# The projection to dt, B and C spread over the in-projection's blocks, and the dt blocks behind the first x and z block

## The reference, cut to what matters

```python
xn = (xf - mu) * rsqrt(var + EPS) * ln_w + ln_b       # LayerNorm over 512 channels
xz = xn @ in_proj_w.T                                 # 512 -> 2 x 1024
xin, z = split(xz, 2)
xs = silu(causal_depthwise_conv(xin, 4 taps) + conv_b)
x_dbl = xs @ x_proj_w.T                               # 1024 -> 32 (dt), 16 (B), 16 (C)
delta = softplus(dt @ dt_proj_w.T + dt_proj_b)        # 32 -> 1024
y = selective_scan(xs, delta, A, B, C, D) * silu(z)
```

## Time and profile before

| | |
|---|---|
| median of 3 executions | 4932.2 us (4929.79 to 4934.46) |
| the profiled execution | 4925.77 us |
| its span, first to last instruction | 4924.1 us |
| mean granted TensorE clock | 0.979 |
| busy share of the span: PE, DVE, ACT, POOL | 94%, 84%, 60%, 69% |
| `front`, about | 95 to 1143 us of the span |
| PE, DVE, ACT, POOL busy in it | 960, 875, 663, 696 us of 1048 |

### The profile page before, as it was taken

How to read it: one execution, slowest core, us unless ns; L and a number is a source line. 1 busy time by engine, 2 the same in 40 slices (tenths; PEclk the granted TensorE clock), 3 DMA queues, 4 the chain that set the end, 5 groups by cost and what they waited for, 6 DMA issues and landing times. The chain is left out here.

```text
span 4924.1 us, 120048 instructions
## 1 busy us (share of the span) xinstructions
PE 4649.7 (94%) x47160; PEld 2945.8 (60%) x47160; DVE 4135.4 (84%) x4348; ACT 2971.5 (60%) x6008; POOL 3377.7 (69%) x1680
## 2 busy tenths in 40 slices
PE   4999999995899999999999999999999899999999
PEld 4666666663455555555555555555554688887787
DVE  7888898887999999999999999999997676776332
ACT  1666666665777767767777777777765454454111
POOL 0577776775999999999999999999997222222000
PEclk9999999997999999999999999999999999999999
DMA  5344334334223332333233323332332111111453
GB/s 201 120 154 150 141 134 150 142 145 163 85 77 96 96 97 79 96 97 96 79 96 99 98 84 96 95 98 79 96 98 76 44 76 77 77 77 75 190 201 139
DMA packets 191786, 538.37 MB, mean 109 GB/s; under 512 B 15824, under 2 KB 15840, under 8 KB 181840
## 3 DMA queue, kind: packets, MB, share of 16 engines
q1 hardware_dynamic: 185920, 480.31, 29.0%
q0 software_dynamic: 5104, 51.35, 2.7%
q10 hardware_dynamic: 288, 0.00, 0.0%
HBM read 329.22 MB, written 202.38 MB: 108 GB/s over the span
## 5 line engine op out<-in xcount | busy, mean ns | idle before, releaser
L975 POOL TENSOR_TENSOR sc_hc<-sc_hc,sc_c_rep 128x1024 f32<-128x1024 f32 x1024 | 2397.4, 2369 | 191.8 <-ACT sc_state L988 189.3
L1176 DVE TENSOR_TENSOR_SCAN sc_hc<-l_m,sc_state,sc_ring 128x512 f32<-128x512 f32 x2048 | 2432.0, 1259 | 32.5 <-PE sc_ring L1099 27.4
L1020 ACT ACTIVATE l_m<-l1s_v,l_neg_a 128x512 f32<-128x512 f32 x2048 | 1351.8, 707 | 2.5 <-issue 1.5
L1099 PEld LDWEIGHTS sc_ring<-sc_diag,l1s_iota 64*64 64x64 f32 x32768 | 890.6, 133 | 703.2 <-issue 703.2
L1099 PE MATMUL sc_ring<-sc_diag,l1s_iota 64*64 64x128 f32 x32768 | 1102.6, 275 | 8.0 <-DVE sc_hc L1176 5.7
L1109 PE MATMUL sc_y_ps<-sc_hc,sc_fold 128*64 128x512 f32 x4096 | 1008.4, 614 | 27.2 <-POOL sc_hc L975 20.9
L988 ACT ACTIVATE sc_state<-sc_hc 128x2 f32<-128x2 f32 x1024 | 206.0, 201 | 647.1 <-DVE sc_hc L1176 647.1
L851 PE MATMUL sc_o_ps<-l1s_et,l_sums 128*128 128x512 f32 x1024 | 560.6, 634 | 8.7 <-ACT l_count L841 8.7
L1431 POOL TENSOR_TENSOR l_count<-l_count,as_oh 128x1024 f32<-128x1024 f32 x64 | 182.4, 2851 | 506.9 <-DVE as_oh L1614 506.9
L1109 PEld LDWEIGHTS sc_y_ps<-sc_hc,sc_fold 128*64 128x64 f32 x4096 | 251.5, 137 | 415.9 <-issue 381.3
L71 PE MATMUL fr_mm<-fr_xn_hi,l0f_w_in_hi 128*128 128x512 f32 x1024 | 436.9, 427 | 26.3 <-DVE fr_delta L675 11.8
(11 more groups left out here) (172 smaller groups left out, 6518.4 us busy)
## 6 DMA issues: line engine op xcount, KB each, us to landing
sc_duz<-spill SPq DMA_DIRECT2D x128, 768.0 KB, 6.0
l1s_v<-spill SPq DMA_DIRECT2D x256, 256.0 KB, 3.9
spill<-fr_z SPq DMA_DIRECT2D x64, 512.0 KB, 2.8
spill<-fr_u SPq DMA_DIRECT2D x32, 1024.0 KB, 8.7
spill<-fr_du SPq DMA_DIRECT2D x32, 1024.0 KB, 4.3
spill<-fr_delta SPq DMA_DIRECT2D x32, 1024.0 KB, 6.4
sc_c_rep<-bc SPq DMA_DIRECT2D x128, 256.0 KB, 4.3
soft<-l1s_et SPq DMA_DIRECT2D x16, 2048.0 KB, 6.2
```

Source lines behind the costliest of these rows:

```text
L975: nc.gpsimd.tensor_tensor(hc[:, p], hc[:, p], c_rep[:, 2 * q:2 * q + 2, :], ALU.mult).then_inc(s_hp, 1)
L1020: nc.scalar.activation(da[:, p % 4, r, :], delta[:, i % 2, p % 2, :], ACT.Exp, scale=keep.neg_a[:, c:c + 1]).then_inc(s_da, 1)
L1099: done = nc.tensor.matmul(to[:, :, k::4], dut[rows, i % 2, k, HALF * h:HALF * h + HALF], diag[rows, u, 4 * q + c:4 * q + 4:2, k, :], start ...
L1176: nc.vector.tensor_tensor_scan(hc[:, p, r, :], da[:, p % 4, r, :], ring[:, SLOT[at], r::2], state[:, i, 2 * p + r:2 * p + r + 1], ALU.mult ...
```

## The change

- PE: `project_x` is cut up. Blocks 0 and 1 are multiplied behind z5, blocks 2 and 3 behind z6, blocks 4, 5 and then 6 behind z7, all in the chunk itself, and block 7 in the next chunk, behind x0. Then z0 is projected, and the d blocks 0 to 3 come behind z0. The order of the PSUM ring follows (x0, z0, d0 to d3).
- ACT: `keep_x` of block 0 goes ahead of `copy_dt`; `silu_z` of block 0 goes ahead of the four `absolute` and of `exp` and `log`.
- DVE: the convolution of block 0 goes ahead of the four `positive`.
- POOL and SP keep their orders.

```diff
-    ORDER = [("x", 0)] + [("d", m) for m in range(4)] + [("z", 0), ("x", 1), ("z", 1), ("x", 2), ("z", 2)]
+    ORDER = [("x", 0), ("z", 0)] + [("d", m) for m in range(4)] + [("x", 1), ("z", 1), ("x", 2), ("z", 2)]
...
             def main(b, j, after, first):
                 g = b * NJ + j
                 ends = after(1) is None or after(1)[0] != b
+                keep_x(g, 0, ends)
                 if not first:
                     copy_dt(g - 1)
-                keep_x(g, 0, ends)
+                silu_z(g, 0)
                 if not first:
                     for m in range(4):
                         absolute(g - 1, m)
                     exp(g - 1, 0)
                     log(g - 1, 0)
-                silu_z(g, 0)
                 keep_x(g, 1, ends)
...
-            def project_x(g):
-                pe.wait_ge(s_dt, g + 1)
-                for m in range(KD):
+            def project_x(g, first, last):
+                if first == 0:
+                    pe.wait_ge(s_dt, g + 1)
+                for m in range(first, last):
                     pe.wait_ge(s_u, KD * g + m + 1 + 2)
-                    last = nc.tensor.matmul(xd_ps[:], keep.w_xp[:, m, :], u[:, m, :], start=(m == 0), stop=(m == KD - 1))
-                last.then_inc(s_xd, 1)
+                    done = nc.tensor.matmul(xd_ps[:], keep.w_xp[:, m, :], u[:, m, :], start=(m == 0), stop=(m == KD - 1))
+                if last == KD:
+                    done.then_inc(s_xd, 1)
 
             def main(b, j, after, first):
                 g = b * NJ + j
+                project(g, "x", 0, first)
                 if not first:
-                    project_x(g - 1)
-                project(g, "x", 0, first)
+                    project_x(g - 1, KD - 1, KD)
+                project(g, "z", 0, first)
                 if not first:
                     pe.wait_ge(s_dt, g + 1)
                     project_dt(g - 1, 0, 4)
-                project(g, "z", 0, first)
                 project(g, "x", 1, first)
...
                     project(g, "z", m, first)
                     if m == 4 and after(1):
                         var(g + 1)
+                    if m > 4:
+                        project_x(g, 2 * m - 10, 2 * m - 8)
+                project_x(g, KD - 2, KD - 1)
...
-            project_x(NG - 1)
+            project_x(NG - 1, KD - 1, KD)
...
             def main(b, j, after, first):
                 g = b * NJ + j
+                conv(g, 0)
                 if not first:
                     for m in range(4):
                         positive(g - 1, m)
-                conv(g, 0)
-                if not first:
                     rounded(g - 1, 0)
```

More of the change, by code:

```diff
@@ L554, in project_dt @@
                                      dt[row:row + RANK + 1, :], start=True,
-                                     stop=True).then_inc(s_mm, {0: 2, 4: 6}.get(m, 1) if ends else 1)
-            def project_x(g):
-                pe.wait_ge(s_dt, g + 1)
-                for m in range(KD):
+                                     stop=True).then_inc(s_mm, {0: 3, 4: 5}.get(m, 1) if ends else 1)
+            def project_x(g, first, last):
+                if first == 0:
+                    pe.wait_ge(s_dt, g + 1)
+                for m in range(first, last):
                     pe.wait_ge(s_u, KD * g + m + 1 + 2)
-                    last = nc.tensor.matmul(xd_ps[:], keep.w_xp[:, m, :], u[:, m, :], start=(m == 0), stop=(m == KD - 1))
-                last.then_inc(s_xd, 1)
+                    done = nc.tensor.matmul(xd_ps[:], keep.w_xp[:, m, :], u[:, m, :], start=(m == 0), stop=(m == KD - 1))
+                if last == KD:
+                    done.then_inc(s_xd, 1)
             def main(b, j, after, first):
                 g = b * NJ + j
+                project(g, "x", 0, first)
                 if not first:
-                    project_x(g - 1)
-                project(g, "x", 0, first)
+                    project_x(g - 1, KD - 1, KD)
+                project(g, "z", 0, first)
                 if not first:
```

## The result

The changed kernel takes 4967.5 us in the median of 4 executions (4965.3 to 4971.0) against 4931.0 us before (4 executions; the three known ahead of the prediction gave 4932.2): a ratio of 1.0079, 95% interval 1.0066 to 1.0092, or +36.5 us. It is slower.

A forecast was written before the change was run, and what follows sets the result against it. The bound was taken to be the loop through POOL, not the 94% busy PE. Terms 27.6 + 3.9 + 8 + 4 = 43.5, less some slack, gave +42 us: 4967.8 us profiled, 4974 us median, range 4938 to 5006 us.

The forecast's parts named there:

- The loop through POOL: Each chunk: POOL, block 7 of u, dt, softplus, POOL; anything between POOL's end and the first d block lengthens it fully.
- D = P + 8.7 in twelve boundaries: First d block's start (D) after POOL's last product ends (P), against P + 6.4; +2.3 us each, 27.6 us.
- The first boundary: Boundary without POOL: products 0 to 3 and switches delay the split and x0; D from 154.03 to 157.9, +3.9 us.
- The boundaries at full clock: Boundaries at 1001 and 1065 us: D from P + 4.6 to about P + 8.6, +4.0 each, 8 us.
- The mean: PE waits 2.4 us instead of 0.33 for the mean; clock falls in one chunk in four, +4 us.
- 0.8 us for switches: PE switching back from products to in-projection matmuls twice more, 0.4 us each at full clock.
- POOL's stretch: POOL's unbroken work per chunk, 49 to 50 us: change 0, bounds -0.4 and +0.5 us a chunk.
- Rival 1: PE is the bound and the change fills its waits: faster, 4910 us, up to -60 us (4872 us); chance 0.11.
- Rival 3: PE waits 3 us or more for the mean every chunk, clock falls twice: +60 us or more; chance 0.20.

The follow-up runs named there:

- e5: Either kernel with the first of POOL's four operations a block left out: kernel before 4841.5 us (ratio 0.9837), changed kernel 4876.0 us (0.9906).
- e3: Kernel before with only products 0 to 6 spread over z5 to z7, product 7 kept at the head: 4927.5 us, ratio 1.0000.
- e2: Kernel before with only z0 and its silu_z moved ahead of the d blocks, all products at the head: 4950.8 us, ratio 1.0048.
- e1: Changed kernel with z0 put back behind the d blocks: 4945.4 us, ratio 1.0038 to the kernel before.
- e6: Kernel before with d blocks 0 to 3 ahead of x0, keep_x and convolution of block 0 behind the softplus work: 4919.1 us, ratio 0.9981.
- e11: Changed kernel with product 7 put back ahead of x0 on PE: 4973.7 us, ratio 1.0095 to the kernel before.
- e4: Changed kernel with five spare fp32 matmuls behind product 6 that nothing reads: 4943.7 us, ratio 1.0035 to the kernel before.
- e7: Kernel before with five spare fp32 matmuls, read by nothing, ahead of product 7: 4935.0 us, ratio 1.0019.

## Why the prediction was right

The forecast was +42 us, 4974 us, with 4938 to 5006 us; it is +36.5 us, 4967.5 us. The mechanism held. The sizes of its terms held less well, and the sum came near because their errors cancel. Point by point:

- *The loop through POOL* is shown: lightening POOL took 86 us off (e5), and in every kernel here D to POOL's start is 9.8 to 10.1 us, so the pause moves with D. Spreading the products alone moved neither D nor the time (e3); z0 (e2) and x0 (e1 against e3) between P and D moved both.
- *D = P + 8.7 in twelve boundaries*: it was P + 9.4 to 9.8. x0 began at P + 0.7 as worked out (P + 0.6), but the low stretch held to the end of x0: 5.0 us, my upper bound, not a mix. The term was 27.6 us. The twelve pauses together grew by 36.4 us, 3.0 us each instead of 2.3 us. The twelve periods from POOL's first start took 819.9 us against 788.4 us, +31.5 us, because POOL's stretches gave 4.9 us back.
- *The first boundary*, +3.9: the mean matmul of chunk 0 stands 2.97 us later already (114.75 against 111.78), before any of the change acts (over thirteen of the traces here it lies between 111.07 and 115.05), and D is 160.77 against 154.03, so +3.8 is the boundary's own.
- *The boundaries at full clock*, +8: the last two periods took 136.4 us against 126.8 us, +9.6. My reason for the old P + 4.6, "because product 7 could start at once", was wrong: product 7 started at P + 0.75 at 1001 us and at P + 0.75 at 476 us alike, and what differed was the clock.
- *The mean*, +4 by a fallen clock: PE waited 1.4 us, not 2.4, and the clock did not fall there. This term is 0. (The working also takes the extra wait once as 1.7 us and once as 2.4 - 0.33 = 2.1 us; it was 1.1 us.) Most of the difference is in the DVE and POOL rows of the changed kernel:

```profile
512.58 1.23 DVE L618 TENSOR_TENSOR fr_half<-l0f_v 128x1024 f32<-128x1024 f32 x1
512.74 2.20 POOL L381 TENSOR_TENSOR fr_du<-fr_du,fr_r 128x512 f32<-128x512 f32 x1 [19.38 <-ACT fr_du L452]
```

  The addition starts 0.16 us ahead of POOL and takes 1.23 us, and POOL's operation takes 2.20 us. Before, the same addition began behind POOL's start and took 2.11 us, and POOL's first operation 1.67 us:

```profile
494.16 2.11 DVE L613 TENSOR_TENSOR fr_half<-l0f_v 128x1024 f32<-128x1024 f32 x1
```

  The Trainium skill (SBUF — State Buffer, section Who interferes with whom) states that a VectorE operation with two SBUF inputs contends with a GpSimd operation that reads SBUF, and that the order in which they are issued decides which of them is blocked; the rows agree.
- *0.8 us for switches* between products and in-projection was nothing: the z7 of the first chunk is 3.4 us later against its mean (6.39 - 2.97), which is 4 x 0.86 and no more.
- *POOL's stretch*: I took 0, with -0.4 to +0.5. It shrank from 49.5 to 48.9 us in most chunks, 0.6 us, a little outside; in the mean of 14 it is 0.34 us, inside.

Sum of the measured terms: 3.8 + 31.5 + 9.6 = 44.9 us for 43.5 predicted. That so little is between them is luck: the pauses grew by 10 us more than the two terms for them said, and the mean (4 us) and POOL's stretches (4.8 us) took it back. The profiled span grew by 43.1 us (3.0 us of late start and some 5 us less in the later stages, which the change does not touch, lie in it too), the medians by 36.5 us, since the profiled execution before lay 5.2 us under its median and the one after 1.4 us over.

Rival 1 (PE is the bound) fell with e3 and e5. Rival 3 (the mean as a second stall) did not occur in the changed kernel. Its condition came nearly true in e2, with 2.6 to 4.0 us of wait for the mean in every chunk and a low clock behind nine of 13, and its price did not: e2 is 23 us slower, not 60 us or more, because that stall lies behind D.

Where I was wrong was in the experiments: I expected 35 to 40 us from z0 alone and got 23, and 33 to 48 us of gain from e6 and got 9, for the same reason. I held the rest of the chunk fixed. A boundary that changes also changes how long PE waits elsewhere, and so the clock, and how early it is at the next boundary.

## What to carry to other kernels

In a software pipeline ask which loop of waits closes from one chunk to the next, and mark on it the point where the late engine ends (P) and the point where its next work is released (D). An instruction moved between the two lengthens each chunk, whatever the busy shares say, by its full time less what the clock gives back (z0: 2.8 us, of which 1.7 us remained in the mean of e2). Useful work moved into a wait ahead of P brings nothing by itself (e3), and it can cost, when it leaves a longer wait right ahead of P and with it a low clock between P and D (e2 against e11). To find whether a 94% busy engine is the bound, make the suspected other one shorter and look at the period; and do not expect the whole of what is cut out of the loop to come back, even where the next engine seems to have slack: in e6 D came 3.4 us earlier where it worked, PE had waited 4.0 us, and still half of the boundaries were late, since the waits of the other engines moved too.

## What was not expected of the hardware

- A 4.4 us wait of PE brought the low clock in each of 14 boundaries, and it held for all 5.0 us of x0; waits of 1.7 to 1.9 us (e2) did at none of eight, waits of 2.0 to 2.1 us (kernel before) at three of four. Five spare matmuls in the wait (e4) were worth 21 to 24 us, where the engine had the slack for them; in the kernel before (e7), with 4.0 us of slack, they cost 7 us.
- The order in which a VectorE and a GpSimd operation start, 0.16 us apart, moves a microsecond from one to the other (1.23 and 2.20 us against 2.11 and 1.67 us).
- A saving at one boundary can be taken back at the next, so that boundaries alternate: in e6 D is mostly P + 2.8 to 3.2 and P + 6.9 by turns, and in e7 P + 4.6 and P + 8.0 to 9.3.
